# One Trainium2 core, attention plus routed experts: normalised rows stored by the router, first layer in two-part weights, one tile fewer

## The reference

```
x  = x + LN(attention(LN(x)))      # 16 heads of 64, keys and values from a latent of 128, causal
f  = LN(x)                         # feats
expert = argmax(f @ centroids.T)   # 8 experts
alpha  = sigmoid(f . centroid[expert])
h  = LN(f) * gamma[e] + beta[e]
y  = f + relu(h @ W1[e].T + b1[e]) @ W2[e].T + b2[e]      # hidden 512
out = x + LN(alpha * y + (1 - alpha) * f)
```

## Time and profile before

| | us |
|---|---|
| median of 3 runs | 1368.81 (1368.3 to 1368.97) |
| the profiled execution, its own time | 1369.18 |
| its span, first to last instruction | 1366.2 |
| busy: PE / DVE / ACT / POOL | 1307.4 / 1188.7 / 1082.8 / 908.9 |
| mean granted TensorE clock, share of full speed | 0.982 |

### The profile page before, as it was taken

The page is one execution under the profiler, slowest core; times in us unless marked ns, Lnnn a source line. Parts: engine busy times, 40 slices in busy tenths (PEclk is TensorE's granted clock), DMA queues, the critical chain, the costliest instruction groups (busy, mean ns, idle before and its releaser), DMA issues.

```text
span 1366.2 us, 34597 instructions
## 1 busy us (share of the span) xinstructions
PE 1307.4 (96%) x9120; PEld 1201.3 (88%) x9120; DVE 1188.7 (87%) x4712; ACT 1082.8 (79%) x3186; POOL 908.9 (67%) x1343
## 2 busy tenths in 40 slices
PE   6999999999999999999999999999999997699993
PEld 5999999999999999999999999999999996588782
DVE  4899999999999999999999999999999884699993
ACT  5988888888888888888888888888888884466661
POOL 3566666666666666666666666666666564288886
PEclk9999999999999999999999999999999998899997
DMA  5000000000000000000000000000000002122220
GB/s 211 5 9 13 12 12 12 12 12 12 12 12 12 12 12 12 12 12 12 11 9 8 11 12 12 12 12 12 12 12 8 8 10 76 42 62 59 60 61 8
DMA packets 38501, 31.83 MB, mean 23 GB/s; under 512 B 4882, under 2 KB 35734, under 8 KB 38080
## 3 DMA queue, kind: packets, MB, share of 16 engines
q1 hardware_dynamic: 31696, 21.47, 5.2%
q0 software_dynamic: 4656, 8.81, 1.9%
q10 hardware_dynamic: 2112, 1.11, 0.3%
HBM read 20.35 MB, written 12.07 MB: 24 GB/s over the span
## 4 chain that ended last, share of the span: by engine, by line
PE 82%; DVE 8%; issue 3%; POOL 3%; DMA 2%; ACT 1%; ACTq 0%; SPq 0%; POOLq 0%; DVEq 0%
PE psS L579 19%; PE psZU L643 13%; PE psZU L628 13%; PE psP L606 12%; PE psZU L631 7%; PE psT L595 5%; PE psT L597 4%; PE psT L596 4%; DVE ff L367 2%; DMA xin<-x 2%; DVE wup_s L384 1%; POOL out L446 1%; DVE on L393 1%; DVE gg L402 1%; PE psM L671 1%
## 5 line engine op out<-in xcount | busy, mean ns | idle before, releaser
L1097 POOL TENSOR_TENSOR prob<-prob,rinv 128x256 f32<-128x256 f32 (+1 forms) x512 | 412.9, 828 | 333.7 <-DVE rinv L858 330.4
L725 ACT ACTIVATE prob<-nscore,nmax 128x128 f32<-128x128 f32 (+1 forms) x1024 | 450.8, 445 | 3.1 <-DVE nmax L840 3.1
L840 DVE CUSTOM_DVE_ANT_0 nscore<-psS,mask 128x128 f32<-128x128 f32 (+1 forms) x1024 | 319.8, 349 | 0.2 <-PE psS L579 0.2
L697 ACT ACTIVATE t_hi<-psT 128x512 fp32r<-128x512 f32 x256 | 153.2, 598 | 151.3 <-PE psT L597 151.3
L827 DVE TENSOR_TENSOR t_lo<-psT,t_hi 128x512 fp32r<-128x512 f32 x256 | 176.5, 689 | 81.7 <-ACT t_hi L697 79.5
L849 DVE TENSOR_TENSOR p_lo<-psP,p_hi 128x768 fp32r<-128x768 f32 x256 | 243.3, 951 | 3.8 <-ACT p_hi L697 3.8
L697 ACT ACTIVATE p_hi<-psP 128x768 fp32r<-128x768 f32 x256 | 208.3, 814 | 6.3 <-PE psP L606 4.1
L606 PE MATMUL psP<-ident,prob 128*128 128x128 f32 x1536 | 209.3, 273 | 0.4 <-DVE p_lo L849 0.4
L863 DVE TENSOR_TENSOR z_lo<-psZU,z_hi 128x512 fp32r<-128x512 f32 x256 | 175.1, 684 | 28.4 <-ACT z_hi L697 14.4
L725 ACT ACTIVATION_READ_ACCUMULATOR prob<-nscore,nmax 128x1 f32 x1024 | 195.0, 190 | 0.0
L579 PE MATMUL psS<-t_lo,xt_hi 128*128 128x256 f32 (+1 forms) x512 | 194.3, 380 | 0.0
(11 more groups left out here) (168 smaller groups left out, 3295.7 us busy)
## 6 DMA issues: line engine op xcount, KB each, us to landing
fin<-routed_rows SPq DMA_DIRECT2D x40, 136.0 KB, 2.2
wx<-ffn_w SPq DMA_DIRECT2D x2, 2058.0 KB, 11.7
xin<-x SPq DMA_DIRECT2D x32, 128.0 KB, 2.2
xres<-x SPq DMA_DIRECT2D x32, 128.0 KB, 2.1
out<-res,fin POOLq DMA_INDIRECT x80, 2.3
routed_rows<-padr ACTq DMA_DIRECT2D x4, 272.0 KB, 4.3
routed_rows<-padr SPq DMA_DIRECT2D x4, 272.0 KB, 5.2
wup_s<-wup SPq DMA_DIRECT2D x1, 1024.0 KB, 5.0
```

Source lines behind the costliest of these rows:

```text
L697: cp = lambda o, i: nc.scalar.activation(o, i, ACT.Copy)
L725: last = nc.scalar.activation(prob[:, pb, h, a:z], nscore[:, (s - lag) % 2, h, a:z], ACT.Exp, bias=nmax[:, pb, h, q:q + 1], scale=-1.0, ac ...
L840: last = v.tensor_tensor_reduce(nscore[:, n1, h, a:z], psQ[q][:, h, :], mask[:, a:z], -1.0, -MASKED, ALU.add, ALU.min, nmax[:, p1, h, q:q ...
L1097: last = g.tensor_tensor(pr, pr, rinv[:, p2, :, q:q + 1].broadcast_to([P, 2, z - a]), ALU.mult)
```

## The change

1. **Rows.** A routed row has 260 floats: the second normalised value nn (128), x after attention (128), the gain alpha times the second reciprocal deviation, an epsilon scaled by that deviation squared, the token's number. f + alpha * y is normalised afterwards, so it may be scaled by the deviation: the expert stage forms nn + gain * y with the scaled epsilon. GpSimd multiplies nn out and the gain and epsilon in the attention slots (r is the slot within the block); alpha is formed there by ACT and DVE. The expert stage loses `ff`, `nn`, the exponential and the sigmoid.
2. **First layer.** PE turns the loaded rows directly. Weights times gamma are kept as high and low parts in float32r (`w1`), made in slots 1 to 8 of the last stretch, one expert a slot, on ACT (high) and DVE (low); ACT copies both parts of an expert for each tile; nt is split too, and the layer is three float32r matmuls for each of the four parts of the hidden layer. The second layer's weights and the biases are copied by themselves.
3. **Order in a slot of the expert stage.** ACT starts with `yt`, then the weight copy, relu, the high part of nt, the second weight copy. DVE starts with `gg` to `gmv` (now one slot later), then relu, `on`, the low part of nt. GpSimd starts with `gve` and `grs`, then `res` of the tile before, and the stores.
4. **39 tiles** instead of 40; the last stretch of slots goes through a part of a round. Buffers are shared with the attention stage (`fin` lies over `prob` and `nscore`), so that loads and copies wait for its end.

The stores themselves (indirect DMAs without accumulation) are as before. The diff, cut to its core:

```diff
-C_RSTD = 128
-C_SHIFT = 129
-C_RSTD2 = 130
-C_SCORE = 131
-C_ID = 132
-ROW = 136
+C_X = 128
+C_GAIN = 256
+C_EPS = 257
+C_ID = 258
+ROW = 260
...
     PAD = 2 * T
     REGION = ntok + T
     TILES = ntok // T + E - 1
-    TILES += -TILES % 8
...
+                if not live(0) and 1 <= s <= E:
+                    act.wait_ge(S["ffnw_loaded"], 5 * 16)
+                    nc.scalar.activation(w1[:, s - 1, 0, :], wx[:, s - 1, 0:FB * P], ACT.Copy,
+                                         scale=gam[:, s - 1:s]).then_inc(S["w1_hi_done"], 1)
...
+                if r == 6 and live_b(2):
+                    act.wait_ge(S["argmax_steps"], 3 * (b0 + db) - 5)
+                    nc.scalar.activation(ea[:], best[:], ACT.Exp, scale=-1.0).then_inc(S["exp_done"], 1)
                 if not live(0) and s == 6:
                     pad(act, range(E // 2, E))
-                if not live(0) and s == 7:
-
-                    act.wait_ge(S["bias_done"], E // 2 + 1)
-                    for e in range(E):
-                        last = nc.scalar.activation(wx[:, e, 0:FB * P], wx[:, e, 0:FB * P], ACT.Copy,
-                                                    scale=gam[:, e:e + 1])
-                    last.then_inc(S["weights_ready"], 1)
...
                 r, db = s % PAIRS, s // PAIRS
+                if not live(0) and 1 <= s <= E:
+                    dve.wait_ge(S["w1_hi_done"], s)
+                    v.scalar_tensor_tensor(w1[:, s - 1, 1, :], wx[:, s - 1, 0:FB * P], gam[:, s - 1:s],
+                                           w1[:, s - 1, 0, :].bitcast(F32), ALU.mult,
+                                           ALU.subtract).then_inc(S["w1_split"], 1)
...
+                    stats(lambda t: pay[:, db, t, C_X:C_X + P], st3, S["st3_done"])
+                if r == 6 and live_b(2):
+
+                    dve.wait_ge(S["exp_done"], b0 + db - 1)
+                    v.tensor_scalar(ea1[:], ea[:], 1.0, None, ALU.add).then_inc(S["alpha_steps"], 1)
+                    dve.wait_ge(S["alpha_steps"], 2 * (b0 + db) - 3)
+                    v.reciprocal(alpha[:], ea1[:]).then_inc(S["alpha_steps"], 1)
...
-                    link(g.tensor_tensor(pay[:, db, :, C_RSTD2], w3[:, 2, :], neg_half[:], ALU.pow))
+                    link(g.tensor_tensor(rstd2[:], w3[:, 2, :], neg_half[:], ALU.pow))
+                if r == 4 and live_b(2):
+
+                    n = b0 + db - 1
+                    wait_apart(pool, S["f_ready"], n)
+                    g.tensor_tensor(pay[:, db, :, 0:P], fn[:], rstd2[:].unsqueeze(2).broadcast_to([P, 2, P]),
+                                    ALU.mult).then_inc(S["nn_stored"], 1)
+                    g.tensor_tensor(sq2[:], rstd2[:], rstd2[:], ALU.mult).then_inc(S["gain_steps"], 1)
+                    pool.wait_ge(S["gain_steps"], 2 * n - 1)
+                    g.tensor_tensor(pay[:, db, :, C_EPS], sq2[:], eps_t[:], ALU.mult).then_inc(S["gain_steps"], 1)
...
-                    wait_apart(pool, S["dest_ready"], b0 + db - 1)
+                    n = b0 + db - 1
+                    pool.wait_ge(S["alpha_steps"], 2 * n)
+                    g.tensor_tensor(pay[:, db, :, C_GAIN], rstd2[:], alpha[:], ALU.mult).then_inc(S["gain_ready"], 1)
+                    wait_apart(pool, S["dest_ready"], n)
+                    pool.wait_ge(S["gain_ready"], n)
+                    pool.wait_ge(S["nn_stored"], n)
+                    pool.wait_ge(S["gain_steps"], 2 * n)
...
-                    pe.wait_ge(S["wst_ready"], m0 + s)
+                    pe.wait_ge(S["w1st_ready"], m0 + s)
...
+                    b = (s - 1) % 2
                     for j in range(FB):
-                        last = mm(psH[:, j, :], wst[:, (s - 1) % 4, j * P:(j + 1) * P], nt[:, (s - 1) % 2, :],
-                                  start=True, stop=True)
+                        for n, (m, nt) in enumerate(((1, nt_hi), (0, nt_lo), (0, nt_hi))):
+                            last = mm(psH[:, j, :], w1st[:, b, m, j * P:(j + 1) * P], nt[:, b, :],
+                                      start=(n == 0), stop=(n == 2))
...
-            act.wait_ge(S["weights_ready"], 1)
+            act.wait_ge(S["w1_split"], E)
+            act.wait_ge(S["z_ready"], PAIRS * NB)
 
             def slot(m0, n0, s, live):
+                if live(3):
+                    act.wait_ge(S["yt_done"], m0 + s - 2)
+                    if live(4):
+                        act.wait_ge(S["y_tr"], m0 + s - 3)
+                    nc.scalar.activation(yt[:], psY[:, 0, :], ACT.Identity,
+                                         bias=bst[:, (s - 3) % 4, FB:FB + 1]).then_inc(S["yt_ready"], 1)
                 if live(0):
-
+                    e = act.value_load(table[0:1, bass.ds(m0 + s, 1), 1], min_val=0, max_val=E - 1)
+                    if live(2):
+                        act.wait_ge(S["h_done"], m0 + s - 1)
+                    nc.scalar.activation(w1st[:, s % 2].rearrange("p m f -> p (m f)"),
+                                         w1[:, bass.ds(e, 1)].rearrange("p a m f -> p (a m f)"),
+                                         ACT.Copy).then_inc(S["w1st_ready"], 1)
...
+                if live(0):
+                    act.wait_ge(S["n_tr"], m0 + s + 1)
+                    cp = lambda o, i: nc.scalar.activation(o, i, ACT.Copy)
+                    cp(nt_hi[:, s % 2, :], psN[:, 0:T]).then_inc(S["nt_hi_done"], 1)
...
-                    e = act.value_load(table[0:1, bass.ds(m0 + s, 1), 1], min_val=0, max_val=E - 1)
-                    nc.scalar.activation(wst[:, s % 4, :], wx[:, bass.ds(e, 1), :].rearrange("p a c -> p (a c)"),
-                                         ACT.Copy).then_inc(S["wst_ready"], 1)
-                    act.wait_ge(f_loaded[s], n0 + 16)
-                    nc.scalar.activation(ea[:, s, :], fin[:, s, :, C_SCORE], ACT.Exp,
-                                         scale=-1.0).then_inc(S["exp_done"], 1)
-                    act.wait_ge(S["n_tr"], m0 + s + 1)
-                    if live(2):
-                        act.wait_ge(S["h_done"], m0 + s - 1)
-                    nc.scalar.activation(nt[:, s % 2, :], psN[:, 0:T], ACT.Copy).then_inc(S["nt_ready"], 1)
...
+                    cp(w2st[:, s % 4, :], wx[:, bass.ds(e, 1), W2:W2 + FB * P].rearrange("p a c -> p (a c)"))
+                    cp(bst[:, s % 4, :], biases[:, bass.ds(e, 1), :].rearrange("p a c -> p (a c)")
+                       ).then_inc(S["w2st_ready"], 1)
...
+                if live(5):
+                    b = (s - 5) % 2
+                    dve.wait_ge(S["grs_ready"], m0 + s - 4)
+                    if live(7):
+                        dve.wait_ge(S["res_ready"], m0 + s - 6)
+                    for t in range(2):
+                        last = v.tensor_scalar(on[:, b, t, :], gg[:, b, t, :], gmv[:, b, t, 0:1], grs[:, b, t:t + 1],
+                                               ALU.subtract, ALU.mult)
+                    last.then_inc(S["on_ready"], 1)
                 if live(0):
-                    dve.wait_ge(S["alpha_steps"], m0 + s + 1)
-                    v.reciprocal(alpha[:, s, :], ea1[:])
+                    dve.wait_ge(S["nt_hi_done"], m0 + s + 1)
+                    v.tensor_tensor(nt_lo[:, s % 2, :], psN[:, 0:T], nt_hi[:, s % 2, :].bitcast(F32),
+                                    ALU.subtract).then_inc(S["nt_ready"], 1)
...
                 if live(4):
-                    m, b, sf = m0 + s - 4, (s - 4) % 2, (s - 4) % FU
+                    m, b, sf = m0 + s - 4, s % 2, (s - 4) % FU
+                    pool.wait_ge(S["gmv_ready"], m + 1)
+                    g.tensor_tensor(gve[:, b, :], gmv[:, b, :, 1], fin[:, sf, :, C_EPS], ALU.add).then_inc(S["gve_done"], 1)
+                    pool.wait_ge(S["gve_done"], m + 1)
+                    g.tensor_tensor(grs[:, b, :], gve[:, b, :], neg_half[:], ALU.pow).then_inc(S["grs_ready"], 1)
+                if live(5):
+                    m, b, sf = m0 + s - 5, (s - 5) % 2, (s - 5) % FU
                     pool.wait_ge(S["on_ready"], m + 1)
-                    if live(6):
-
-                        pool.wait_ge(stored[(s - 6) % FU], n0 + n0 + (32 if s >= 6 else 0))
-                    g.tensor_tensor(res[:, b], on[:], fin[:, sf, :, 0:P], ALU.add).then_inc(S["res_ready"], 1)
-                if live(3):
-                    m3, b3 = m0 + s - 3, (s - 3) % 2
-                    pool.wait_ge(S["gmv_ready"], m3 + 1)
-                    g.tensor_tensor(gve[:], gmv[:, b3, :, 1], eps_t[:], ALU.add).then_inc(S["gve_done"], 1)
-                    pool.wait_ge(S["gve_done"], m3 + 1)
-                    g.tensor_tensor(grs[:, b3, :], gve[:], neg_half[:], ALU.pow).then_inc(S["grs_ready"], 1)
-                if live(4):
+                    if live(7):
+                        pool.wait_ge(stored[(s - 7) % FU], n0 + n0 + (32 if s >= 7 else 0))
+                    g.tensor_tensor(res[:, b], on[:, b], fin[:, sf, :, C_X:C_X + P], ALU.add).then_inc(S["res_ready"], 1)
                     wait_apart(pool, S["res_ready"], m + 1)
```

(65 more changed lines are left out.)

125 lines of the change are left out of this document (53 added, 72 removed).

## The result

The changed kernel takes 1399.43 us (median of 4 runs, 1399.14 to 1400.73), the kernel before, run beside it, 1368.55: a ratio of 1.023 (95% interval [1.0212, 1.0247]), slower. The forecast was 1395.0. The profiled execution took 1399.52 us with a span of 1397.7, against 1369.18 and 1366.2.

The account below looks back on a forecast made before the run. The prediction took TensorE to bound the attention stage and GpSimd the expert stage; 4.3 between the stages, 2.7 filling and 19.2 steady gave +26.2 us, so 1395.0 us, range 1384 to 1410.

Parts of the forecast that it names:

- After the change every tile has the last tile's order: GpSimd, expert stage: stores directly follow the residual add, so a gap of 0.85 us replaces 0.19 in every tile.
- The forecast of 4.87 per tile: GpSimd's pace in the expert stage: 4.21 + 0.66 = 4.87 us per tile, 4.80 to 4.95 with scatter.
- The term of +19.2: Expert stage, first store to last tile's first store: 184.1 us against 164.9, the saved tile included.
- Rival A: Expert stage: the stores' preparation stays hidden, gap 0.19, pace 4.21, 1369.2 us, not slower; 8%.
- Between the stages: Attention to expert stage: padding delays weight pieces and last-block statistics; first first-layer matmul +4.3 us, bounds 0 and +10.
- the bound of +10: Between the stages: the upper bound if the padding, 1.9 times the bytes, takes twice as long to issue.
- still lands before the table is done: Between the stages: the last row store, about 1.0 behind the sigmoid, was to land before DVE's table is done.
- Filling: Start of the expert stage, first first-layer matmul to first store: +2.7 us on 18.6, range 0 to +5.
- The wider fills at the start I cost at nothing: the loads hide them: Kernel start: the wider fills add 0 us, since the loads hide them.
- B: Rival A, and slot 7 between the stages not held up by the padding, statistics still near 1146: 1363.2 us; 4%.
- C: Expert stage: DVE's ring takes over, 4.5 us with one residual add in it, 5.3 with two; 1410 us; 10%.
- D: Expert stage: TensorE's clock drops, its 3.8 us a tile would be 7.6; +104 us, 1499 us; 3%.

Follow-up runs that it names:

- kernel 1: Changed kernel with GpSimd's residual add back ahead of epsilon and power, nothing else: 1378.11 us, ratio to the kernel before 1.0068.
- kernel 3: Changed kernel with each tile's two stores issued one slot later, the add still behind the power: 1376.34 us (one run).
- kernel 2: The kernel before with the new order alone (epsilon and power, then residual add and stores): 1397.29 us, ratio 1.0208.
- kernel 5: Changed kernel with weight pieces 4 to 7 moved to slot 9 on ScalarE and slot 12 on VectorE: 1395.91 us, ratio 1.0199.
- kernel 4: Changed kernel with weight pieces 5 to 7 moved up from slots 6 to 8 into slots 5 and 6: 1398.91 us, ratio 1.022.
- kernel 6: Changed kernel with 40 tiles again instead of 39, so the loop of eight ends without the odd remainder copy: 1401.92 us (one run).
- 7: kernel 3 with the epsilon add moved from GpSimd to VectorE behind its statistics: 1366.45 us (one run).
- 8: Changed kernel with stores a slot later, epsilon add on VectorE, late weight pieces, padding fills behind the constants: 1363.96 us, ratio to the kernel before 0.9963.

## Why the prediction held, point by point

- **The order.** "After the change every tile has the last tile's order" is shown from both sides: kernels 1 and 3 take the order out of the changed kernel and win 21 to 23 us, kernel 2 puts it into the kernel before and loses 28. The forecast of 4.87 per tile rested on one gap at the last tile, 0.86; measured were 0.87 and a tile of 4.91. The term of +19.2 came out as 21.5: 38 times 0.04 is 1.5 of that, and the one step where the loop ends lasts 5.75, 0.84 over the others (0.77 over them in the kernel before). The forecast had put no step of that kind into its 38.
- **Rival A** is out at its own point of decision, 0.87 against 0.19. The Trainium skill (Perfetto Trace Analysis, DMA Instruction — SWDGE (GPSIMD)) has a store decoded and pushed into a wait queue before its own semaphores are met. The prediction said that the trace differs from this rule, but the rows do not test it: `wait_apart` puts the wait for the add into an instruction of its own ahead of the store, and what the rows show is that wait clearing at 1251.6 and the moves behind it. Whether a store that carries its wait itself would hide its preparation, no run tried.
- **Between the stages** the mechanism was right, and shown by kernel 5: ScalarE's padding, its piece, VectorE's half, then the statistics. "GpSimd's epsilon moves to 1155.4": 1156.34, with the stretch beginning 1.6 later. The issue of the padding, 1.9 times the bytes, took 5.12 us and not more than the 5.87 before, so the bound of +10 stayed far. The net of +4.3 measured 4.75, and one step in it failed: the last row store "still lands before the table is done". The table was done at 1172.22 + 0.18 = 1172.40, the row store landed at 1170.61 + 3.05 = 1173.66 (its step in the chain that ended last), and SyncE's first load waited for it (us in total, times, longest):

  ```profile
SPq L247 <- DMA routed_rows<-pay,dst: 0.7, 1, 0.7
  ```

  From the start of the table's last instruction to that of the first load pass 1.67 us, against 1.01 before; the forecast had put no difference there. What the prediction didn't see either is the second queue behind VectorE: on GpSimd the last block's epsilon add stands behind the row stores of the block before, so that pulling the pieces forward (kernel 4) gave back almost nothing.
- **Filling**, +2.7: measured +1.3 between the first matmul and the first store, but this is one execution. Kernel 6, with the same code up to there (its table has 40 entries), took 21.6 us, +3.0. What differs in the rows is TensorE's granted clock, columns as in the earlier trace rows, the changed kernel first and kernel 6 second:

  ```profile
1182.00:1186.00 4.00, 2.93 (x20) 2.80 (x21) 1.68 (x5) 3.32 (x9) 0.00 (x0) 1.00 0.60 173
  ```

  ```profile
1182.00:1186.00 4.00, 4.00 (x19) 3.78 (x19) 1.30 (x3) 1.94 (x6) 0.00 (x0) 0.63 0.23 69
  ```

  Both began the first layer at the lower of the clock's two levels (1.2 GHz). TensorE was busy 3.35 and 2.76 us of the 4 before this stretch; then the clock was full at 1182 in the changed kernel, some 3 us after its first matmul, and only inside 1184 to 1185 in kernel 6, some 8 us after. Of the kernels that store in the same slot, kernels 1 and 4 rose as early and took 20.1 and 19.9 us, kernel 5 rose 7 to 8 us after and took 21.3. So the term of +2.7 lies inside what the same code gives, and the +1.3 owes something to an early rise.
- **"The wider fills at the start I cost at nothing: the loads hide them"** failed in part. The fill of the padding tile went from 0.55 to 0.96 us on GpSimd, with one more small fill behind it, and the constants that TensorE's transposes wait for moved from 13.89 to 14.73, 0.27 of it ahead of the fills and 0.57 by them. Two rows of the changed kernel's timeline of GpSimd:

```profile
13.31 0.96 POOL L1015 MEMSET padr<- 128x1040 f32 x1
...
14.73 0.19 POOL L1019 CAST idf<-iota_i 128x2 f32<-128x2 int32 x1
```

  The mark at the end of the attention stage stood 1.6 later; over the five kernels with this start and these pieces it lay between 1146.0 and 1148.5, against 1144.8 and 1146.0 for the two with the old start, so about 1.8 in the mean. That the fills make all of it is not shown: their own part at the start is the 0.57, and kernels with the same start lie up to 2.5 apart.
- **The tail**, +2.3, was in no term. Between the two profiled executions the forecast is off by 1399.52 - 1395.4 = 4.1 us: start +1.6, between the stages +0.45, filling -1.4, steps +2.3, tail +2.3, outside the span -1.2. That the sum came nearer than its parts is luck: they miss by 6.7 us upwards and by 2.6 downwards.
- **Rivals B, C and D.** The statistics ran at 1155.41 and not near 1146 (B). VectorE was stretched, but had room: 35.30 of 50 us (C). The granted clock was 1.00 in the steady stretch, with TensorE busy 41.59 of 50 us (D).

## What to carry to other kernels

In this kernel an indirect store of GpSimd left 0.7 us of preparation open (0.87 for 0.19) where its wait was met directly ahead of it; with another instruction of that engine between the producer and the store (kernel 1), or with the store a turn later (kernel 3), the step went from 4.91 back to 4.29 and 4.22. When several engines look full in a steady stage, find the one whose idle time is only its own gaps, and read what stands in the gap: here one reordering of three lines weighed more (21 to 23 of 31 us) than all else in the change, taken net. Work moved "into idle slots" must be placed by what is queued behind it on both its own engine and the next one: two more pieces ahead of the destinations cost about as much as two behind the padding.

## What was not expected of the hardware

The end of the span has a price of its own: 9.2 to 9.3 us from the last store's start in five kernels (the kernel before, 2, 6, 7 and 8) and 11.6 to 11.8 in the other five. Each of the five long ones has two fetches of instructions in its last 14 us, none of the short ones has any.

VectorE's two normalisations of a tile lasted 0.60 us where they ran beside power and stores (kernel 1) and 1.01 where GpSimd's residual add started with them. By groups, changed kernel first, kernel 1 second (duration in ns min/median/max):

```profile
L411 DVE TENSOR_SCALAR xres<-xin,gmv,grs x76: 334/340/759, 1199.7 to 1380.1; 128x128 f32<-128x128 f32 x76
```

```profile
L411 DVE TENSOR_SCALAR xres<-xin,gmv,grs x76: 334/345/419, 1200.2 to 1358.3; 128x128 f32<-128x128 f32 x76
```

One of a pair started at 1250.90, 0.05 behind the start of the add that ran to 1251.57, and lasted 0.75, to 1251.65, just behind the add's end. The add that uses the result starts at 1255.76, so the step lost nothing by it. The Trainium skill (SBUF — State Buffer, SBUF: two separate sides) has the two engines share one pair of ports, which an instruction of GpSimd or one of certain kinds on VectorE holds as a lock from its start to its end. A VectorE instruction that ends with the add agrees with this.
